# Moving the last routing group behind a second pair of shared-expert work in a fused embed, attention and mixture-of-experts kernel

## The reference, cut to what matters

```
h   = concat([token, patches @ W.T + b] + pos, ngram_embeddings(x_txt))      # (64, 229, 128)
h   = h + attn(layernorm(h))          # gated attention, squared relu of q k^T + w
t   = layernorm(h).reshape(-1, 128)   # 14656 tokens
shared = sum over 2 shared experts of gelu(t @ sw1.T + sb1) @ sw2.T + sb2     # F = 512
probs  = softmax(t @ gate_w.T + gate_b)      # 8 experts
top_v, top_i = top_k(probs, 2)
routed = sum over the 2 chosen experts e of top_v * (gelu(t @ rw1[e].T + rb1[e]) @ rw2[e].T + rb2[e])
out = h + shared + routed
```

## Time and profile before

| | us |
|---|---|
| median of 3 runs | 1212.78 (1212.64 to 1215.49) |
| the profiled execution, its own time | 1205.45 |
| span of its trace | 1203.7 |
| granted TensorE clock, mean | 0.992 |
| TensorE busy | 1158.8 (96%) |
| VectorE busy | 972.5 (81%) |
| ScalarE busy | 806.5 (67%) |
| GpSimd busy | 844.1 (70%) |

### The profile page before, as it was taken

The page is one execution under the profiler, slowest core; times in us unless marked ns, Lnnn a source line. Parts: engine busy times, 40 slices in busy tenths (PEclk is TensorE's granted clock), DMA queues, the critical chain, the costliest instruction groups (busy, mean ns, idle before and its releaser), DMA issues.

```text
span 1203.7 us, 31970 instructions
## 1 busy us (share of the span) xinstructions
PE 1158.8 (96%) x9446; PEld 874.6 (73%) x9446; DVE 972.5 (81%) x2516; ACT 806.5 (67%) x1867; POOL 844.1 (70%) x808
## 2 busy tenths in 40 slices
PE   7999999999999999979989999999999999999998
PEld 4777777777777777845545559999999999965555
DVE  5788998888888888888967777777777777779997
ACT  2566666666765666746545547777777777768887
POOL 5446776666677777678877846777777777776664
PEclk9999999999999999989999999999999999999999
DMA  7233444444444442234344324454444554549998
GB/s 216 71 122 118 126 122 136 135 136 126 129 138 143 134 136 83 88 101 102 105 119 130 98 47 99 98 98 100 92 97 99 92 97 90 92 86 198 207 194 171
DMA packets 208055, 143.51 MB, mean 119 GB/s; under 512 B 119036, under 2 KB 186745, under 8 KB 207892
## 3 DMA queue, kind: packets, MB, share of 16 engines
q1 hardware_dynamic: 166868, 93.93, 31.0%
q0 software_dynamic: 36992, 40.97, 15.8%
q10 hardware_dynamic: 4032, 6.57, 2.2%
HBM read 70.38 MB, written 55.96 MB: 105 GB/s over the span
## 4 chain that ended last, share of the span: by engine, by line
POOL 39%; issue 25%; PE 24%; DVE 4%; ACT 3%; DMA 2%; SPq 1%; POOLq 0%; ACTq 0%; DVEq 0%
POOL y_dram L1645 9%; POOL slots_dram L490 9%; POOL slots_dram L1634 6%; POOL rstd L531 4%; POOL rstd L537 3%; POOL slots_dram L500 3%; PE bank L1929 2%; PE bank L1953 2%; PE bank L1952 2%; PE bank L1954 2%; PE bank L1931 2%; PE bank L1930 2%; POOL emb L460 2%; PE bank L1394 2%; PE bank L1396 2%
## 5 line engine op out<-in xcount | busy, mean ns | idle before, releaser
L1645 POOL DMA_INDIRECT y_dram<-y_sb,y_row x244 | 268.7, 1101 | 92.8 <-issue 73.5
L1728 ACT ACTIVATE gel_all<-bank,b 128x256 f32<-128x256 f32 x488 | 191.8, 475 | 36.6 <-PE bank L1931 33.9
L1361 ACT ACTIVATE gel_all<-bank,b 128x458 f32<-128x458 f32 x256 | 154.9, 640 | 91.1 <-PE bank L1355 63.5
L1952 PE MATMUL bank<-w_part_hi,hid_all 128*128 x976 | 170.6, 219 | 0.0
L1954 PE MATMUL bank<-w_part_hi,hid_all 128*128 x976 | 169.7, 219 | 0.0
L1953 PE MATMUL bank<-w_part_lo,hid_all 128*128 x976 | 169.7, 219 | 0.0
L1850 DVE CAST hid_all<-gel_all 128x1024 f16<-128x1024 f32 x122 | 85.2, 698 | 93.6 <-ACT gel_all L1728 93.6
L490 POOL DMA_INDIRECT slots_dram<-row_bufs,slot_1st x128 | 131.9, 1031 | 40.6 <-issue 38.2
L1852 DVE TENSOR_TENSOR hid_all<-gel_all,hid_all 128x1024 f16<-128x1024 f32 x122 | 149.5, 1226 | 4.2
L1372 DVE TENSOR_TENSOR hid_all<-gel_all,hid_all 128x916 f16<-128x916 f32 x128 | 142.4, 1113 | 4.4
L1634 POOL DMA_INDIRECT slots_dram<-row_bufs,slot_2nd x96 | 119.4, 1243 | 29.9 <-issue 28.7
(11 more groups left out here) (193 smaller groups left out, 3003.3 us busy)
## 6 DMA issues: line engine op xcount, KB each, us to landing
xin<-in_xmain SPq DMA_DIRECT2D x32, 771.8 KB
x2r_dram<-row_bufs SPq DMA_DIRECT2D x32, 260.0 KB, 2.1
x2t_dram<-x2T SPq DMA_DIRECT2D x32, 229.0 KB, 2.9
x_cols<-x2t_dram ACTq DMA_DIRECT2D x28, 229.0 KB
row_bufs<-x2r_dram SPq DMA_DIRECT2D x24, 260.0 KB, 2.9
stage<-in_ffn_w SPq DMA_DIRECT2D x20, 256.0 KB
xin<-in_xrest SPq DMA_DIRECT2D x32, 128.6 KB
y_dram<-y_sb,y_row POOLq DMA_INDIRECT x244
```

The source lines that it names most:

```text
L1361: act.activation(self.gel[:, f // 2 % 2, f % 2, :], self.up_dst(k, f), ACT.Gelu, bias=self.b1[:, f:f + 1]).then_inc(self.gel_ready, 1)
L1645: pool.indirect_dma_start(out=y_dram, in_=y_sb[:, s, c, :], in_offset=None, out_offset=bass.IndirectOffsetOnAxis(ap=y_row[:, s, c:c + 1], ...
L1728: act.activation(gel[:, s8 % 2, f, :], up_bank[s8 % 2][half][:, (f % 2) * TILE:(f % 2 + 1) * TILE], ACT.Gelu, bias=of_expert(b1, SHARED * ...
L1952: pe.matmul(part, h_hi, w2_hi, start=False, stop=False)
```

## The change

Three things move. On VectorE, `top` and `choose` of the last group now come after split 3 of pair 0 and split 0 of pair 1, and `slots` after splits 1 and 2 of pair 1. On TensorE the ranking comes after the rest of pair 1 and after up groups 0 and 1 of pair 2, down group 0 of pair 1 and the transposes of pair 0. The subtraction for the exponentials, Exp itself and the copy to the tags come after pair 2 on VectorE and ScalarE, with the tags of the blocks one pair later (slot 2i-6+f//4, block 0 still right after Exp). ScalarE's wait for the stores of `x2t_dram` moves with them.

```diff
             between(dve, 2)
+            between(dve, 3)
+            between(dve, 4)
             top(b, 1)
             choose(GROUPS - 1)
-            between(dve, 3)
+            between(dve, 5)
+            between(dve, 6)
             slots(GROUPS - 1, 1, 16 * (b - 3))
...
             between(pe, 4)
+            between(pe, 5)
             rank(GROUPS - 1)
-            between(pe, 5)
+            between(pe, 6)
...
         def scalar(act):
...
-                        for n in due(2 * i - 4 + f // 4):
-                            if n < PAIRS - AGAIN:
+                        for n in due(2 * i - 6 + f // 4):
+                            if 0 < n < PAIRS - AGAIN:
                                 tag_rows(n, n % ROWS_BUFS)
...
+            pair(2)
             act.wait_ge(centred, 2)
             act.activation(expd, expd, ACT.Exp).then_inc(exps, 1)
             for parity in range(2):
                 act.wait_ge(done.t_out[parity], 16 * PAIRS // 2)
...
             act.wait_ge(tags_up, 1)
             tag_rows(0, 0)
-            for i in range(2, EARLY_PAIRS):
+            for i in range(3, EARLY_PAIRS):
                 pair(i)
...
         def vector_between(dve, part):
-            early.split(dve, 0, 0, part)
+            early.split(dve, part // NJ, part // NJ, part % NJ)
...
-            for j in range(2):
-                early.split(dve, 1, 1, j)
+            early.split(dve, 1, 1, NJ - 1)
+            pair(2, 0)
             dve.wait_ge(done.top_kept, PAIRS)
             dve.tensor_tensor(expd, top8[:, :, :], top8[:, :, 0:1].to_broadcast([P, NCH, 8]),
                               ALU.subtract).then_inc(centred, 1)
-            for j in range(2, NJ):
-                early.split(dve, 1, 1, j)
             dve.wait_ge(exps, 2)
             dve.tensor_copy(tag_2nd[:, 4 * AGAIN:, 1], expd[:, 4 * AGAIN:, 1]).then_inc(tags_up, 1)
-            pair(2, 0)
             after(dve.reduce_sum(weight_1st[:, :], expd, axis=AXX))
...
-        def tensor_pair(pe, i, parity):
-            for f in range(NG):
+        def tensor_pair(pe, i, parity, parts=range(NG)):
+            for f in parts:
...
                     if f % 2 == 1:
                         early.down(pe, 0, f // 2)
+                tensor_pair(pe, 2, 0, range(0, 2))
+            elif part == 6:
+                tensor_pair(pe, 2, 0, range(2, NG))
...
-            pair_loop(pe, pair, 2, EARLY_PAIRS)
+            pair_loop(pe, pair, 3, EARLY_PAIRS)
```

More of the change, by code:

```diff
@@ L1680, in scalar @@
         def scalar(act):
[L1681 to L1684, removed]
             def tag_rows(n, b):
@@ L1706, in pair @@
                     early.load(act, i + 2, i % 2)
+            pair(2)
+            act.wait_ge(centred, 2)
+            act.activation(expd, expd, ACT.Exp).then_inc(exps, 1)
+            for parity in range(2):
+                act.wait_ge(done.t_out[parity], 16 * PAIRS // 2)
             act.wait_ge(tags_up, 1)
             tag_rows(0, 0)
-            for i in range(2, EARLY_PAIRS):
+            for i in range(3, EARLY_PAIRS):
                 pair(i)
```

## The result

The changed kernel took 1216.45 us (median of 20 runs, 1211.27 to 1220.28). The kernel before, run beside it, took 1209.38 us (20 runs, 1203.33 to 1215.49). The ratio is 1.0054, with an interval of 1.0039 to 1.0070. So the change costs about 6.5 us by the ratio (7.1 by the two medians), where a gain of 1.4 us was forecast. The median of 1212.78 us that the forecast stood on was of 3 runs; against 1209.38 the same forecast would have been some 1208.

A forecast was written before the change was run, and what follows sets the result against it. TensorE was taken to bound the kernel, its routed tiles starting once early pairs and tile 0's load were done. A gain of 1.4 us made the profiled 1205.45 us 1204.0; plus 7.33 gave 1211.4 us, range 1207.3 to 1216.8.

The forecast's parts named there:

- The first hole goes: TensorE before the last group's ranking: the 4.75 us wait and about 2.5 us of slow clock go, net gain 5.0 us.
- The slots come later: GpSimd: scatters of pair 30 begin near 544.0, 2.2 us later (bounds 0.6 and 3.3), with all later scatters behind them.
- The exponentials: TensorE near 555 idles 4.4 us against 0.70, then a slow clock: cost 3.7 + 2.5 us, bounds 2 and 9.
- The tags: Later tags remove most ScalarE waits for rows: 5.5 us gained on TensorE, bounds 3 and 6.4; GpSimd shifts about 3.5.
- The slower rival: In the 96 scatters, block 1's tag starves GpSimd: shift 8.6 us, end 4.5 us later, 1217.3 us; chance 0.17.
- The sum up to tile 0: Start of routed tiles: TensorE through at 710, tile 0 loaded at 710.0 and ready at 714.4, 1.9 us earlier.
- The 2.0 us from the memset: Before tile 0, VectorE's last casts finish before GpSimd's memset, sparing TensorE 2.0 us, bounds 0 and 4.3.

The follow-up runs named there:

- Experiment 3: Kernel before, with three stores one after the other on SyncE between the last scatter and the first tile load: 1216.34 us, ratio 1.0062.
- experiment 4: Changed kernel, with SyncE reading the bases of the first 12 tiles early, while it waits for the last scatters: 1207.70 us, ratio 0.9982 to the kernel before.
- experiments 2: Changed kernel with the last group's routing put back, so only exponentials and tags come a pair later: 1217.82 us, ratio 1.0074 to the kernel before.
- experiment 6: Kernel before, with SyncE reading the base twice for every fourth tile: 1224.11 us, ratio 1.0122.
- experiments 1 and 7: Changed kernel with Exp and tags put back, only routing moved: 1208.16 us, ratio 1.0003; the same with 12 tile bases read early: 1207.09 us, ratio 0.9987.

## Why the prediction was wrong

**The first hole goes: right.** The ranking followed the transposes that started at 542.36 (forecast 542.2). The slots (L799 on VectorE) were there at 544.35, forecast 543.8. The new waits were 1.24 and 1.10 us, forecast 1.4 and 0.9, and the slow clock at the ranking went.

**The slots come later: the size was somewhat low.** The scatters of pair 30 began at 545.24, 3.4 us later than before and not 2.2; the bound was 3.3. This scatter started 0.9 us behind the slots (544.35 to 545.24), which the sum did not have.

**The exponentials: right in kind, priced too high.** The subtraction started at 553.49 and ended at 554.71 (forecast 554.0), the second load ended at 557.78, GELUs resumed at 557.79 (forecast 558.4), and TensorE got its bank at 558.49 (forecast 559.1). It was idle 3.10 us, not 4.4: it ran dry 0.7 us later than forecast, and Exp's table load (1.28) ran at 551.26, ahead of the wait for VectorE, where the forecast had put it behind. The slow clock cost about 1.7 us, not 2.5: the granted clock was 0.85 from 556 to 560 and 0.73 from 560 to 564, and (0.15 + 0.27) x 4 = 1.7. By these terms the part cost 2.4 + 1.7 = 4.1 us instead of 6.2. TensorE began pair 4 at 564.84, 0.2 us earlier than before and not 1.2 later.

**The tags: the cure was partial, the shift right by luck.** ScalarE's waits for rows fell from 18.0 to 11.4 us; under 8 was forecast. TensorE began pair 17 at 696.35 instead of 699.45, so from pair 4 on it had won 2.9 us, not 5.5. GpSimd's shift was 559.69 - 555.96 = 3.7 us at the first scatter and 708.39 - 704.28 = 4.1 at the memset, forecast 3.5. But the 3.5 was 2.2 from the slots and 1.3 from a late tag of block 1. The slots alone gave 3.4, and the tag of block 1 (written at 563.83, its first scatter at 565.94) held nothing up: two errors that cancelled. The slower rival, in which that tag starves GpSimd, needed a shift of 5.4 and did not happen. The kernel is slower by another mechanism than the one that had the 0.17.

**The sum up to tile 0: right, with some luck.** The 2.0 us from the memset came: the last matmul of the 18 pairs started at 710.98 instead of 716.06, 5.1 us earlier, after 3.1 at pair 17. TensorE was through near 711.3 (714.33 - 3.00; forecast 710). The first load came at 710.57 (forecast 710.0), 0.6 us late, and from there to the use of tile 0 it took 3.8 us (forecast 4.4), 0.6 us less, so tile 0 started at 714.33 (forecast 714.4). The first routed down group stood at 720.67, forecast 721.0; the 5.3 us that the forecast put between it and tile 0 follows from no row (722.41 - 1.25 - 716.25 is 4.9). By the forecast's own account the change had gained 1.9 us at tile 0.

**The step that failed** is the last of the sum: "of which nothing is lost in the tiles, since TensorE bounds them". From the first matmul of tile 0 to that of the last tile TensorE took 1067.45 - 714.33 = 353.1 us instead of 337.9. The row was read as "TensorE is the bound". It says only that TensorE had work. The two rows of SyncE, tiles loaded 2.68 us apart, served for the spacing of the first tiles only. They were not set beside TensorE's pace of 2.79, nor was the chain followed over all tiles, where it averages 2.82. So the 9.8 us between first load and use, which the sum treated as slack to be spent, was what kept TensorE fed. Experiment 3 took it away and got the loss; experiment 4 rebuilt it and the loss went. That also explains why the slip was invisible at tile 0: in the changed kernel the end followed the last load, not the first use. From the last load to the end of the span it is 155.5 us after. It is 155.9 before, though no tile was late there: of its head start too not much was left at the last tile (6.3 us, against 5.6 after).

**The range.** 1216.45 lies inside 1207.3 to 1216.8, and that is luck twice over. The upper part of the range stood for the rival that did not happen, and the whole range stood on a median of 3 runs that was 3.4 us above that of 20. Moved down by 3.4, it would have ended at 1213.4.

**Profiled against timed.** The profiled execution of before lies 3.9 us below the median of its kernel, that of after 2.6 above, so 13.6 holds a chance share, and the timed 6.5 us is the cost. By parts, the 13.6 are 4.1 (first load) plus 9.9 (the chain of 121 steps, 351.3 against 341.4 us) less 0.4. Of the 9.9, 9.3 is the duration of SyncE's two issues, summed over the 121 steps: 213.8 us in the execution before and 223.1 after. The sum varies with the same issues in the stream, but perhaps not by chance alone. It was 220.3 to 223.1 us in the changed kernel and experiments 2 and 3, where the head start was gone from the first tile on, and 213.7 to 217.2 in the seven others. Against a link speaks experiment 6, with 215.8 though TensorE waited 13 times. Whether a short head start itself stretches the issues stays open.

**On the rules.** The second table load again was followed by its GELU 0.01 us after its end, with no drain between them, so the drain that the Trainium skill (ScalarE: Activation LUTs, section What ACT_TABLE_LOAD costs) adds did not appear. The last cast of VectorE ended at 706.44, ahead of the memset, as the sum had it. The price of an issue was the term to look at. For a transfer from GpSimd the Trainium skill (DMA: Bandwidth & Descriptors, section Anatomy of one DMA — SWDGE (gpsimd) path) puts some 50 ns of the fixed cost on the sequencer's dispatch and most of it on the receipt of the write. That is no figure for SyncE's path. On SyncE here the issue alone took 0.42 us for a plain load and some 1.2 or more for a transposing one, and that is what the tiles ran into.

**Open.** Why the transposing issue is stretched to as much as 2.5 us in some tiles was not tried. Nor was why the 96 scatters take 144.9 to 149.1 us from one execution to another; the two with the routing half alone, experiments 1 and 7, were the shortest (144.9 and 146.3).

## What to carry to other kernels

A busy share of 100% says that an engine was fed, not how much was in reserve. Before a head start is spent, follow the feeding queue's own pace over the whole stage, register reads and issues included, and compare it with the consumer's: here 2.82 against 2.79 us, and over 122 tiles that used up 3.5 us of head start. Where a queue's engine idles ahead of such a stage, let it read its addresses there; that took an edit of two lines here, and no loss was left that could be measured.

## What the runs showed of the hardware

The issue of a transposing load on SyncE is neither cheap nor steady. Start times aside, one line of the trace by source gives least, median and greatest duration in ns, for the changed kernel:

```profile
L1579 SPq DMA_TRANSPOSE xT_r<-slots_dram x122: 1211/1226/2499, 710.6 to 1061.8; - x122
...
L1574 SPq TENSOR_LOAD <-tile_base x122: 263/286/537, 709.9 to 1060.7; - x122
```

With the read, the tags' 0.42 us and the gaps between, tiles followed 2.54 us apart at best (713.26 to 715.80), and 2.90 on average.

In this kernel a table load did not stand behind the wait of the instruction that it serves. At 551.26 it ran as soon as ScalarE was free, 3.48 us before Exp, which waited for VectorE. So a late operand cost less than wait plus load.
